# Transposed scores in blocks of 64 keys, masked on the tensor engine, and v weighted in 64x32 tiles

## The chip, the core and the metric

The kernel runs on one core of a Trainium2 chip. The core has a tensor engine (PE) that multiplies matrices out of SBUF into the banks of PSUM, a vector engine (DVE), a scalar engine (ACT), a general engine (POOL), a queue that issues transfers (SP), and 16 DMA engines. All run on their own and wait for each other by semaphores. The metric is the device time of one launch in microseconds, lower is better.

## What is computed

One transformer block over 8 batches of 512 tokens with 128 features: layer norm, then causal attention with 16 heads of 8 features, and beside it a mixture of 8 experts (2 per token, 176 hidden features each) with a shared expert of 352 hidden features. All sums are added to the tokens.

```python
xn = _layernorm(x, axis=-1)
# attention, H = 16 heads of 8 features, S = 512
q, k, v = (to_heads(q), to_heads(k), to_heads(v))
scores = jnp.einsum('bhqd,bhkd->bhqk', q * scale, k) + causal_bias
attn = jax.nn.softmax(scores, axis=-1)
out = jnp.einsum('bhqk,bhkd->bhqd', attn, v) ... @ w_out.T + b_out
# experts: top 2 of 8 by softmax of xn @ gate_w.T, weights scaled by 2.5
g = jax.nn.silu(jnp.einsum('td,edf->etf', x, w_gate)) * jnp.einsum('td,edf->etf', x, w_up)
y = jnp.einsum('te,etd->td', combine, jnp.einsum('etf,efd->etd', g, w_down))
return x + attention(xn) + y + shared(xn)
```

## The kernel before

Each engine has its instructions written out in a fixed order. The batches 1 to 6 are a loop on each engine, batch 0 and 7 are written beside it. A batch `b` has two stages, which the engines pass one after the other:

**The expert stage** (`experts_and_maxima`) has 14 tiles of hidden features, `k` = 0 to 13. For each tile PE computes gate and up (`gate_up`, 6 matmuls of 512 columns, L537 to L539), ACT the silu (L871), POOL the routing weight (L1016), DVE the product (`hidden`, L1229), ACT and POOL the split into two parts (L878, L1024), and PE `down` (3 matmuls, L553 to L555). Between the tiles stand 18 units `pair(b, n)`: scores of queries by keys in 64x64 tiles of the array (`head_scores`, L573), with the causal mask added on PE by 4 more matmuls (`mask_scores`, L564), from which DVE takes the negative row maximum (`maxima`, L1253). Units 0 to 6 share one pair of PSUM banks, so that unit n+1 waits for the maximum of unit n. The maxima go into the operand `q_op` as further rows, so that the transposed scores come out with the maximum subtracted. At `k` = 2 and 3 stand the pieces that end the attention of the batch before: `transpose_o` (L684), `normalise_o` (L1298, L1300), `transpose_on` (L691), `project_out` (L697), `add_attention` (L1315).

**The attention stage** (`attend`). PE computes the scores transposed, keys by queries (`scores_t`, L646), in units of two PSUM banks, 1024 columns of 128 rows. There are 4 groups of 4 heads with 5 units each, 20 in all. A unit has 2 or 4 matmuls in 64x128 tiles: two heads in the two halves of the rows, 128 keys, and the queries from the first of these keys to 511. ACT takes the exponential of each unit from PSUM to `probs` in SBUF (L934). The units alternate between two pairs of banks, so that unit n waits for the exponential of unit n-2. POOL sets the entries above the diagonal of each 128x128 block to zero (`mask`, L1044, 4 instructions per group). Then PE weights v (`weigh_v`, L673): 4 steps per group, one per block of keys, in the order 512, 384, 128, 256 queries; each step has 4 matmuls in float32 in 128x32 tiles, one head each. One group is weighted behind the scores of the next. A float32 matmul is two instructions in the trace.

The end of the stage overlaps the start of the next: `pair(b+1, 0)` waits for the last exponential but one, `gate_up(b+1, 0)` for the last one, since its banks are those of the scores. On PE the last steps of `weigh_v` stand between `pair` 0, `gate_up` 0, `pair` 1, `gate_up` 1 and `pair` 2. In the same stage PE projects q, transposes y, the routing weights (L510) and the first half of the output (`transpose_o(i, 0)`), and DVE splits q and k, computes the routing weights, takes and normalises the first half of the output (`take_o(i, 0)`, L1291, and `normalise_o(i, 0)`) and adds the last batch's attention.

v and the router's logits of the next batch are projected at the end of the expert stage (`project_v_and_logits`, L503): 4 matmuls with 128x128 weights and 136 columns.

## Time and profile before

| | |
|---|---|
| median of 3 runs | 576.67 us (576.14 to 577.02) |
| profiled execution, its own time | 575.52 us |
| span of the profiled execution | 573.8 us |
| PE busy | 522.2 us (91%) |
| DVE busy | 452.5 us (79%) |
| ACT busy | 344.8 us (60%) |
| POOL busy | 322.3 us (56%) |
| granted clock of PE | 0.994 |

The page gives busy times over the whole span. The two stages have different limits, so that the stages are read apart. From 148 us on the kernel repeats itself: the first exponential of a batch starts at 210.27 us and that of the next batch at 276.99 us, so a batch takes 66.72 us. The rows below are mostly from this one batch. In a timeline row the numbers are the start and the length in us; the distance from one start to the next on PE is what a piece costs, since the recorded lengths of matmuls overlap.

### The profile page before, as it was taken

To read this page: it belongs to the slowest core of one execution; us is meant where nothing else is said; L and a number is where in the kernel's file an instruction comes from. 1 tells how busy PE (TensorE), PEld (TensorE's weight loads), DVE (VectorE), ACT (ScalarE), POOL (GpSimd) and SP (SyncE) were. 2 spreads that over 40 slices of the span, in tenths; PEclk is the share of its full clock that TensorE was granted. 3 is DMA by queue.
4 is the path that set the end of the run, shared out by engine and by line. 5 is a ranking of instruction groups with operands and counts; after the bars stand their busy time and mean duration, and the time that the engine had idled before them with its cause. 6 is when DMAs were issued, how large, how long until landed. Compare 5 with 4: busy or idle time off the path is not lost.

```text
span 573.8 us, 13133 instructions
## 1 busy us (share of the span) xinstructions
PE 522.2 (91%) x4536; PEld 295.5 (51%) x4536; DVE 452.5 (79%) x852; ACT 344.8 (60%) x463; POOL 322.3 (56%) x345
## 2 busy tenths in 40 slices
PE   2679999989999999999999999999999999999985
PEld 1345633656346752576436662466525764366522
DVE  5989798897869968797868968699687978589604
ACT  6422597355963479434983469634794349734693
POOL 2036743775447835479255864478355782558552
PEclk9899999999999999999999999999999999999999
DMA  8984037500475006900268004740069003580001
GB/s 269 267 221 114 12 125 206 132 2 9 146 198 138 2 11 194 261 22 0 104 181 200 0 9 153 220 104 0 22 184 261 18 0 119 164 207 1 10 1 37
DMA packets 45405, 61.99 MB, mean 108 GB/s; under 512 B 4960, under 2 KB 28992, under 8 KB 45376
## 3 DMA queue, kind: packets, MB, share of 16 engines
q1 hardware_dynamic: 42668, 58.37, 36.2%
q10 hardware_dynamic: 2708, 3.24, 1.9%
q8 instruction: 18, 0.29, 0.2%
q14 instruction: 11, 0.09, 0.1%
HBM read 45.21 MB, written 15.34 MB: 106 GB/s over the span
## 4 chain that ended last, share of the span: by engine, by line
PE 60%; DVE 13%; ACT 11%; issue 8%; POOL 5%; DMA 2%; ACTq 1%; POOLq 0%; DVEq 0%
PE banks L673 10%; ACT probs L934 8%; PE banks L537 7%; PE banks L538 6%; PE banks L539 6%; PE banks L573 6%; PE banks L553 6%; PE banks L646 6%; DVE neg_max L1253 5%; PE banks L555 3%; PE banks L554 3%; POOL hid_lo L1024 2%; DVE probs L1229 2%; POOL probs L1044 1%; POOL probs L1016 1%
## 5 line engine op out<-in xcount | busy, mean ns | idle before, releaser
L1253 DVE TENSOR_REDUCE neg_max<-banks 128x2 f32<-128x1024 f32 (+7 forms) x240 | 178.3, 794 | 17.2 <-PE banks L564 16.8
L934 ACT ACTIVATE probs<-banks 128x1024 f32<-128x1024 f32 x160 | 155.4, 1031 | 11.4 <-PE banks L646 9.2
L1044 POOL TENSOR_SCALAR_AFFINE_SELECT probs<-probs 128x512 f32<-128x512 f32 x128 | 90.8, 732 | 124.0 <-ACT probs L934 124.0
L1016 POOL TENSOR_TENSOR probs<-probs,cb 128x512 f32<-128x512 f32 x88 | 113.2, 1286 | 81.4 <-ACT probs L871 80.9
L871 ACT ACTIVATE probs<-banks 128x512 f32<-128x512 f32 (+1 forms) x112 | 67.0, 598 | 134.2 <-PE banks L539 133.9
L1024 POOL TENSOR_TENSOR hid_lo<-probs,hid_hi 128x512 fp32r<-128x512 f32 x85 | 109.6, 1290 | 36.6 <-ACT hid_hi L878 36.3
L1229 DVE TENSOR_TENSOR probs<-probs,banks 128x512 f32<-128x512 f32 (+1 forms) x112 | 76.4, 683 | 35.8 <-POOL probs L1016 27.7
L537 PE MATMUL banks<-x_hi,w_hi 128*128 128x512 f32 (+1 forms) x224 | 95.0, 424 | 4.4 <-DVE probs L1229 4.4
L673 PE MATMUL banks<-probs,v_op 128*32 128x512 f32 (+3 forms) x1024 | 95.2, 444 | 3.7 <-POOL probs L1044 3.5
L538 PE MATMUL banks<-x_lo,w_hi 128*128 128x512 f32 (+1 forms) x224 | 89.0, 398 | 0.0
L539 PE MATMUL banks<-x_hi,w_lo 128*128 128x512 f32 (+1 forms) x224 | 88.8, 396 | 0.0
L878 ACT ACTIVATE hid_hi<-probs 128x512 fp32r<-128x512 f32 (+1 forms) x96 | 60.4, 629 | 43.4 <-DVE probs L1229 43.3
L646 PE MATMUL banks<-q_op,k_op 64*128 64x384 bf16 (+3 forms) x512 | 62.8, 302 | 11.6 <-ACT probs L934 11.3
L573 PE MATMUL banks<-k_op,q_op 64*64 64x448 bf16 (+7 forms) x1024 | 54.2, 293 | 9.8 <-DVE neg_max L1253 7.0
L553 PE MATMUL banks<-hid_hi,wd_hi 128*128 128x512 f32 (+1 forms) x112 | 55.3, 493 | 4.2 <-POOL hid_lo L1024 3.6
L646 PEld LDWEIGHTS banks<-q_op,k_op 64*128 64x128 bf16 x512 | 17.4, 94 | 79.9 <-ACT probs L934 57.4
L537 PEld LDWEIGHTS banks<-x_hi,w_hi 128*128 128x128 f32 (+1 forms) x224 | 42.0, 187 | 20.6 <-DVE probs L1229 5.4
L539 PEld LDWEIGHTS banks<-x_hi,w_lo 128*128 128x128 f32 (+1 forms) x224 | 42.0, 188 | 10.7
L538 PEld LDWEIGHTS banks<-x_lo,w_hi 128*128 128x128 f32 (+1 forms) x224 | 42.1, 188 | 7.8 <-issue 0.2
L573 PEld LDWEIGHTS banks<-k_op,q_op 64*64 64x64 bf16 x1024 | 21.0, 105 | 46.8 <-issue 44.6
L555 PE MATMUL banks<-hid_lo,wd_hi 128*128 128x512 f32 (+1 forms) x112 | 44.7, 399 | 0.0
L554 PE MATMUL banks<-hid_hi,wd_lo 128*128 128x512 f32 (+1 forms) x112 | 44.4, 396 | 0.0
(136 smaller groups left out, 552.3 us busy)
## 6 DMA issues: line engine op xcount, KB each, us to landing
cb<-c_dram SPq DMA_DIRECT2D x31, 256.0 KB, 3.9
q_op<-q_dram SPq DMA_DIRECT2D x15, 512.0 KB, 6.8
k_op<-k_dram SPq DMA_DIRECT2D x15, 512.0 KB, 8.2
cb<-c_dram SPq DMA_DIRECT2D x16, 224.0 KB, 4.3
q_dram<-q_parts SPq DMA_DIRECT2D x8, 384.0 KB, 2.5
k_dram<-k_parts SPq DMA_DIRECT2D x8, 384.0 KB, 2.5
cb<-c_dram SPq DMA_DIRECT2D x16, 192.0 KB, 4.2
cb<-c_dram SPq DMA_DIRECT2D x15, 160.0 KB, 4.3
```

The lines of the kernel that those rows point to most:

```text
L537: pe.matmul(bank, w_hi[:, w, cols], x_hi[:, :], start=True, stop=False)
L538: pe.matmul(bank, w_hi[:, w, cols], x_lo[:, :], start=False, stop=False)
L539: pe.matmul(bank, w_lo[:, w, cols], x_hi[:, :], start=False, stop=True).then_inc(ready, 1)
L553: pe.matmul(bank_y[:, :], wd_hi[0:n, tile, :], hi, start=(k == 0), stop=False)
L573: pe.matmul(bank[rows, a, at:at + n], q_op[own, 2 * g + c, HALF * jq:HALF * (jq + 1)], k_op[own, 2 * g + c, 0:n], start=first, stop=False, ...
L646: mm = pe.matmul(bank[:, at:at + S - kb * P], k_op[r:r + HALF, h // 2, kb * P:(kb + 1) * P], q_op[r:r + HALF, h // 2, kb * P:S], start=Tru ...
L673: mm = pe.matmul(bank[32 * j:32 * j + 32, kb * P:S], v_op[:, kb, g % 2, 4 * (g // 2) + j, :], probs_of(g, j, kb), start=(c == 0 and g % 2 ...
L934: nc.scalar.activation(probs[:, g % 2, 2 * u:2 * u + 2, :], ring[:, at:at + 2, :], ACT.Exp).then_inc(exp_done, 1)
L1016: nc.gpsimd.tensor_tensor(sg[k % 3][:, :], sg[k % 3][:, :], cb[:, tiles_of(b)[k], :], ALU.mult).then_inc(weighted, 1)
L1024: nc.gpsimd.tensor_tensor(hid_lo[0:n, k % 3, :], hid[k % 3][0:n, :], hid_hi[0:n, k % 3, :].bitcast(F32), ALU.subtract).then_inc(hid_lo_don ...
L1044: return nc.gpsimd.affine_select(out=view, in_=view, compare_op=ALU.is_ge, fill=0.0, base=0, pattern=[[0, 4], [1, P]], channel_multiplier=-1)
L1253: return nc.vector.tensor_reduce(out, in_, AX.X, ALU.max, negate=True)
```

## The change

Transposed scores. A unit now holds 64 keys instead of 128 for each head, for two pairs of heads at once, in 64x64 tiles: (a, c) are the halves of the array's rows and columns, and 4 heads of one group lie in one unit of two banks. Key blocks w and 8-w share a unit, so a group has 4 units, and every two groups share a ninth: 18 units per batch instead of 20, of 1024 columns each as before. A unit has 4 or 8 matmuls and then 4 more that add the causal mask (`mask_scores_t`). POOL's masking (L1044) is gone, with its semaphore.

Weighting v. A step is one block of 64 keys for the 8 heads of two groups: 8 matmuls in 64x32 tiles, 4 in each half of the rows, into both output banks. The widths of the 8 steps of two groups are 512, 448, 64, 384, 128, 320, 192 and 256 queries, 16 steps per batch as before. A step follows two score units behind the one that holds its keys. `probs` is a ring of 12 units instead of two buffers of 10 blocks.

What follows from this. v is projected with the two halves of the heads in the two halves of the columns (16 matmuls of 128x64 weights and 64 or 72 columns instead of 4), and placed by POOL in 2 copies instead of 4. Both halves of the output are complete only after the last step, so `take_o(i, 0)`, `transpose_o(i, 0)` and `normalise_o(i, 0)` move to the places of their second halves, and `transpose_on` moves behind `gate_up(b, 3)`. The last batch ends with both halves in `last_take_o`, `last_transpose_o` and `last_normalise_o`. The weights of v, the bias of v and the output weights are loaded with 2, 1 and 4 more transfers. `att` shares the memory of `o_norm`.

```diff
+ST_ALL = NAT_ALL
+WEIGHINGS = OWN_UNITS + 1
+PV_ALL = GROUPS // 2 * WEIGHINGS
+WEIGH_BEHIND = 2
+FIRST_WEIGHING = 4
...
-                for a in range(2):
-                    bank = ring[:, 2 * ((n + 1) % 2) + a, :]
...
-                    for h, kb, at in parts:
-                        r = half(h)
-                        mm = pe.matmul(bank[:, at:at + S - kb * P],
-                                       k_op[r:r + HALF, h // 2, kb * P:(kb + 1) * P],
-                                       q_op[r:r + HALF, h // 2, kb * P:S], start=True, stop=True)
+                apart(pe, pe_passed)
+                blocks = keys_of(n)
+                for m, (g, jk, at) in enumerate(blocks):
+                    for c in range(2):
+                        for a in range(2):
+                            pe.matmul(ring[half(c), 2 * ((n + 1) % 2) + a, at:at + S - HALF * jk],
+                                      k_op[half(a), 2 * g + c, HALF * jk:HALF * (jk + 1)],
+                                      q_op[half(a), 2 * g + c, HALF * jk:S], start=(m == 0), stop=False,
+                                      tile_position=(HALF * a, HALF * c), skip_group_check=True)
+                for c in range(2):
+                    for a in range(2):
+                        mm = mask_scores_t(ring[half(c), 2 * ((n + 1) % 2) + a, :], a, c, blocks)
...
-                for j in range(4):
-                    mm = pe.matmul(bank[32 * j:32 * j + 32, kb * P:S], v_op[:, kb, g % 2, 4 * (g // 2) + j, :],
-                                   probs_of(g, j, kb), start=(c == 0 and g % 2 == 0), stop=(c == 3 and g % 2 == 1),
-                                   tile_position=(0, 32 * j), skip_group_check=True)
+                for c in range(2):
+                    for j in range(4):
+                        x, a = j // 2, j % 2
+                        mm = pe.matmul(nat[32 * j:32 * j + 32, c, HALF * jk:S], v_op[half(c), jk ^ c, t, j, :],
+                                       probs[half(c), 2 * home_of(units[x]) + a, at[x]:at[x] + S - HALF * jk],
+                                       start=(t == 0 and jk == 0), stop=(t == 1 and jk == JQ // 2),
+                                       tile_position=(HALF * c, 32 * j), skip_group_check=True)
...
-                for q in range(QT):
-                    mm = pe.matmul(vl[:, q // 2, q % 2, :], xnT[:, q * P:(q + 1) * P], wvg_sb[:, :],
-                                   start=True, stop=True)
+                for jk in range(JQ):
+                    for c in range(2):
+                        at = jk ^ c
+                        n = VG if at % 2 == 0 else E // 2
+                        mm = pe.matmul(vl[half(c), at // 4, at % 4, 0:n], xnT[:, jk * HALF:(jk + 1) * HALF],
+                                       wvg_sb[:, c, 0:n], start=True, stop=True, tile_position=(0, HALF * c),
+                                       skip_group_check=True)
...
                     if k == 2:
+                        transpose_o(i, 0)
                         transpose_o(i, 1)
+                    if k == 3:
+                        transpose_on(i)
...
                     if k >= 2:
                         down(b, k - 2, i)
-                    if k == 2:
-                        transpose_on(i)
...
-            def mask(view):
...
-                return nc.gpsimd.affine_select(out=view, in_=view, compare_op=ALU.is_ge, fill=0.0, base=0,
-                                               pattern=[[0, 4], [1, P]], channel_multiplier=-1)
...
                     if k == 2:
+                        normalise_o(i, 0)
                         normalise_o(i, 1)
                     for m in range(PAIRS_AT[k]):
                         if k == 1 and m == 1:
+                            take_o(i, 0)
                             take_o(i, 1)
```

Three places show how the instructions move; the names are those of the two sources, and their line numbers differ. The first is PE at the end of the attention stage in the loop. Before, in the older source's lines, with L646 the transposed scores, L673 the weighting of v and L573 with L564 the first unit of the next batch's maxima:

```order
L646 MATMUL banks<-q_op,k_op 128x256 x4
L664 REGISTER_ALU
L673 MATMUL banks<-probs,v_op 32x512 x4
L664 REGISTER_ALU
L673 MATMUL banks<-probs,v_op 32x384 x4
L588 ISA
L596 REGISTER_ALU
L573 MATMUL banks<-k_op,q_op 64x512 x4
L564 MATMUL banks<-mask_half,ident_half 64x64 x4
```

And the same place after, where L683 and L696 are the transposed scores and their mask, L713 the weighting, L615 and L606 the maxima's unit:

```order
L683 MATMUL banks<-q_op,k_op 64x256 x8
L696 MATMUL banks<-ident_half,mask_half 64x2x64 x4
L713 MATMUL banks<-probs,v_op 32x128 x8
L630 ISA
L638 REGISTER_ALU
L615 MATMUL banks<-k_op,q_op 64x512 x4
L606 MATMUL banks<-mask_half,ident_half 64x64 x4
```

Two long steps of weighting (512 and 384 queries) stood between the last scores and the next batch's first unit; now one short step does. The second place is PE behind `gate_up(b, 0)`. Before:

```order
L539 MATMUL banks<-x_hi,w_lo 128x512
L664 REGISTER_ALU
L673 MATMUL banks<-probs,v_op 32x128 x4
L601 ISA
L573 MATMUL banks<-k_op,q_op 64x448 x4
L573 MATMUL banks<-k_op,q_op 64x64 x4
L564 MATMUL banks<-mask_half,ident_half 64x128 x4
```

After:

```order
L581 MATMUL banks<-x_hi,w_lo 128x512
L713 MATMUL banks<-probs,v_op 32x320 x8
L713 MATMUL banks<-probs,v_op 32x192 x8
L702 REGISTER_ALU
L713 MATMUL banks<-probs,v_op 32x256 x8
L643 REGISTER_ALU
L615 MATMUL banks<-k_op,q_op 64x448 x4
```

Three steps stand there where one did, and the step of 256 queries that stood behind `gate_up(b, 1)` is gone. The third place is DVE in tiles 1 and 2 of the expert stage, with the maxima (L1253), the copy of the output (L1291) and its normalisation (L1298, L1300). Before:

```order
L1290 REGISTER_ALU
L1291 COPY o_sb<-banks 128x512
L1249 REGISTER_ALU
L1253 TENSOR_REDUCE neg_max<-banks 128x2 x2
L1223 REGISTER_ALU
L1229 TENSOR_TENSOR probs<-probs,banks 128x512
L1297 REGISTER_ALU
L1298 RECIPROCAL o_rden<-banks 128x32
L1300 TENSOR_TENSOR o_norm<-banks,o_rden 128x16x16
```

After, where the same operations are L1311, L1273, L1249, L1319 and L1321:

```order
L1310 ISA
L1311 COPY o_sb<-banks 128x512 x2
L1269 REGISTER_ALU
L1273 TENSOR_REDUCE neg_max<-banks 128x2 x2
L1243 REGISTER_ALU
L1249 TENSOR_TENSOR probs<-probs,banks 128x512
L1317 ISA
L1319 RECIPROCAL o_rden<-banks 128x32
L1321 TENSOR_TENSOR o_norm<-banks,o_rden 128x16x16
L1317 REGISTER_ALU
L1319 RECIPROCAL o_rden<-banks 128x32
L1321 TENSOR_TENSOR o_norm<-banks,o_rden 128x16x16
```

Two copies and two normalisations stand where one of each did; the first of each has left the attention stage.

## Rows read from the trace of the kernel before

**Rows 1.** ACT's timeline in one batch; [idle before it <- who ended it]
```profile
210.27 1.02 ACT L934 ACTIVATE probs<-banks 128x1024 f32<-128x1024 f32 x1 [0.57 <-PE banks L646]
213.99 0.70 ACT L849 ACTIVATE qk_f<-banks,bq_scaled 128x512 f32<-128x512 f32 x1
214.56 14.70 ACT L934 ACTIVATE probs<-banks 128x1024 f32<-128x1024 f32 x15
229.51 1.94 ACT L934 ACTIVATE probs<-banks 128x1024 f32<-128x1024 f32 x2 [0.24 <-PE banks L646]
```

**Rows 2.** PE's timeline, one group of five score units inside the attention stage
```profile
220.52 0.39 PE L646 MATMUL banks<-q_op,k_op 64*128 64x512 bf16 x2 [0.46 <-ACT probs L934]
220.84 1.06 PE L673 MATMUL banks<-probs,v_op 128*32 128x512 f32 x8
221.83 0.39 PE L646 MATMUL banks<-q_op,k_op 64*128 64x512 bf16 x2
223.26 0.42 PE L673 MATMUL banks<-probs,v_op 128*32 128x128 f32 x8
223.62 0.40 PE L646 MATMUL banks<-q_op,k_op 64*128 64x384 bf16 x4
```

**Rows 3.** PE's timeline from the last scores to the second tile's gate
```profile
231.86 0.85 PE L673 MATMUL banks<-probs,v_op 128*32 128x384 f32 x8 [0.50 <-POOL probs L1044]
232.64 0.41 PE L573 MATMUL banks<-k_op,q_op 64*64 64x512 bf16 x4
233.01 0.50 PE L537 MATMUL banks<-x_hi,w_hi 128*128 128x512 f32 x1
234.60 0.43 PE L673 MATMUL banks<-probs,v_op 128*32 128x128 f32 x8
234.96 0.41 PE L573 MATMUL banks<-k_op,q_op 64*64 64x448 bf16 x8
235.36 0.50 PE L537 MATMUL banks<-x_hi,w_hi 128*128 128x512 f32 x1
```

**Rows 4.** PE's timeline, tiles 2 to 4
```profile
239.41 0.60 PE L684 MATMUL banks<-ident_sb,o_sb 128*128 128x128 f32 x4
242.21 0.41 PE L573 MATMUL banks<-k_op,q_op 64*64 64x512 bf16 x4 [0.48 <-DVE neg_max L1253]
246.76 0.50 PE L537 MATMUL banks<-x_hi,w_hi 128*128 128x512 f32 x1
```

**Rows 5.** DVE's timeline in tile 2
```profile
240.05 0.35 DVE L1298 RECIPROCAL o_rden<-banks 128x32 f32<-128x32 f32 x1
240.78 1.28 DVE L1253 TENSOR_REDUCE neg_max<-banks 128x2 f32<-128x640 f32 x2
```

**Rows 6.** PE's timeline, two units for the maxima in a row
```profile
248.35 0.41 PE L573 MATMUL banks<-k_op,q_op 64*64 64x320 bf16 x8
248.65 0.39 PE L573 MATMUL banks<-k_op,q_op 64*64 64x256 bf16 x8
```

**Rows 7.** PE's timeline, the projection of v and what follows it
```profile
275.54 1.09 PE L503 MATMUL banks<-wvg_sb,xnT 128*128 128x136 f32 x8
276.56 0.39 PE L646 MATMUL banks<-q_op,k_op 64*128 64x512 bf16 x2
```

**Rows 8.** The last batch's end, timelines of ACT, PE and DVE
```profile
545.60 15.61 ACT L934 ACTIVATE probs<-banks 128x1024 f32<-128x1024 f32 x16
563.81 1.81 PE L673 MATMUL banks<-probs,v_op 128*32 128x384 f32 x24 [0.51 <-POOL probs L1044]
565.69 0.76 DVE L1332 COPY o_sb<-banks 128x256 f32<-128x256 f32 x2 [2.43 <-PE banks L673]
```

**Rows 9.** SP's timeline at the start; the last row is from the list of transfers
```profile
2.40 0.43 SPq L345 DMA_DIRECT2D wvg_sb<-in_gateT  x1
6.47 1.28 SPq L352 DMA_DIRECT2D probs<-in_ident  x2
...
probs<-in_ident SPq DMA_DIRECT2D x2, 16.0 KB, 7.0
```

More of the change, by code:

```diff
@@ L189, in block_kernel @@
         ident_f = early[:, after + HALF:after + 2 * HALF]
[L191 to L192 removed]
+        hid = [probs[:, 2 * n, :] for n in (LEFT - 2, LEFT - 1, LEFT - 3)]
+        sg = [probs[:, 2 * n + 1, :] for n in (LEFT - 2, LEFT - 1, LEFT - 3)]
         yT = o_sb[:, 0, :]
@@ new lines, in scores_t @@
+                apart(pe, pe_passed)
+                blocks = keys_of(n)
+                for m, (g, jk, at) in enumerate(blocks):
+                    for c in range(2):
+                        for a in range(2):
[3 more added lines that the diff above has]
+                                      tile_position=(HALF * a, HALF * c), skip_group_check=True)
@@ new lines, in scores_t, with mask_scores_t @@
+                for c in range(2):
+                    for a in range(2):
+                        mm = mask_scores_t(ring[half(c), 2 * ((n + 1) % 2) + a, :], a, c, blocks)
+                mm.then_inc(st_ready, 1)
+            def mask_scores_t(bank, a, c, blocks):
+                second = blocks[-1][2] // HALF
+                diagonal = bank.rearrange("p (k n) -> p k n", n=HALF)[:, 0:second + 1:max(second, 1), :]
+                return pe.matmul(diagonal, mask_half[half(a), :],
+                                 ident_half[half(a), :].unsqueeze(1).to_broadcast([HALF, len(blocks), HALF]),
+                                 start=False, stop=True, tile_position=(HALF * a, HALF * c), skip_group_check=True)
@@ new lines, in weigh_v @@
+            def weigh_v(i, t, w, part, front):
+                pe.wait_ge(exp_done, ST_ALL * i + last_unit_of(t, w) + 1)
+                if t == 0 and w == 0 and part == 0:
+                    pe.wait_ge(v_placed, i + 1)
+                    if front:
+                        pe.wait_ge(q_done, i + 2)
+                        pe.wait_ge(k_done, i + 2)
+                apart(pe, pe_passed)
+                jk, units, at = weighing_of(t, w)[part]
+                for c in range(2):
+                    for j in range(4):
[4 more added lines that the diff above has]
+                                       tile_position=(HALF * c, 32 * j), skip_group_check=True)
+                if part == len(weighing_of(t, w)) - 1:
@@ L863, in silu @@
                 if k == 0:
-                    before(act, pv_done, 0 if isinstance(b, int) and b == 0 else GROUPS * b - 1)
+                    before(act, pv_done, 0 if isinstance(b, int) and b == 0 else PV_ALL * b - WEIGHINGS)
                 act.wait_ge(gate_ready, NT * b + k + 1)
@@ L904, in experts @@
                             take_xT(b + 1)
+                    if k == 3 and i is not None:
+                        act.wait_ge(onT_ready, i + 1)
+                        nc.scalar.activation(o_normT[:, :], nat[:, 0, :], ACT.Copy).then_inc(onT_done, 1)
                     if i is None and k == 1:
@@ L911, in experts @@
                         square_root(1)
-                    if k == 2 and i is not None:
-                        act.wait_ge(onT_ready, i + 1)
-                        nc.scalar.activation(o_normT[:, :], nat[:, 0, :], ACT.Copy).then_inc(onT_done, 1)
             def take_y(i):
```

261 lines of the change are left out of this document (119 added, 142 removed).

## Prediction

> **What bounds the kernel now.** I read the busy times first. PE is busy 91% of the span, but a busy PE is not one whose speed counts in each stage, so the timelines of one batch come next, one engine after the other. In the attention stage ACT's row of fifteen exponentials takes 14.70 us, 0.98 us each with no gap, and before it ACT waits little [rows 1]. PE waits for ACT once in each group of five score units, 0.46 us here [rows 2]. So ACT sets the pace there, with PE close behind: a group takes five exponentials, 4.9 us, and with one wait of 0.46 us in it PE has 4.4 us of work. At the end of the stage it is not ACT any more. The last exponential ends at 231.45 [rows 1], while the first gate matmul, which needs nothing else of ACT, starts at 233.01: a wait of 0.50 us for POOL's mask, a step of weighting and the first unit for the maxima stand before it on PE [rows 3]. In the expert stage PE and DVE are both full. PE waits for DVE once, 0.48 us, at the unit of the maxima in tile 2 [rows 4]. So a batch of 66.72 us has about 1.9 us of ACT's pace to gain from two exponentials less, some 1.5 us at the end of the stage, and little cover for new PE or DVE work.
>
> **Scores and their mask.** Before, a unit costs PE 0.32 us (220.52 to 220.84) [rows 2]. After, a unit is the same set of instructions as a unit for the maxima, 4 or 8 matmuls in 64x64 tiles and 4 for the mask, which costs 0.37 and 0.40 us with the change of tiling in it (232.64 to 233.01, 234.96 to 235.36) [rows 3]; without that change it is 0.30 [rows 6]. Of 18 units 4 are short: 4 x 0.37 + 14 x 0.40 = 7.1 us per batch against 20 x 0.32 = 6.4, so +0.7. The cost is well covered by rows, the lower end would be 18 x 0.30 = 5.4.
>
> **Weighting v.** Before, a step of 512 queries costs 0.99 us (220.84 to 221.83) and one of 128 costs 0.36 (223.26 to 223.62) [rows 2]: 1.64 ns per query and 0.15 us fixed. A batch has 4 x 1280 = 5120 queries in 16 steps, 8.4 + 2.4 = 10.8 us. After, a step has 8 matmuls in 64x32 tiles. No row shows float32 in such tiles. If all eight stream at once, as the four of a unit for the maxima do, the cost per query stays, and there are 2 x 2304 = 4608 queries in 16 steps. I take 0.17 us fixed, near the 0.15 of the nearest row and a little more for twice the instructions: 7.6 + 2.7 = 10.3 us, so -0.5. The lower end is 0.05 fixed (the change of tiling nearly free, -1.9 more), the upper ends are rivals 2 and 3 below.
>
> **The attention stage.** What counts is when the last exponential ends. The fifth score unit starts at about 214.7, beside the fourth exponential (214.56) [rows 1]. From there to the end of the last scores PE now has 14 units (12 x 0.40 + 2 x 0.37 = 5.54), 12 steps with 3712 queries (6.09 + 12 x 0.17 = 8.13) and the turning of the routing weights (0.3): 13.97 us, to 228.7. With 0.2 us to ACT and 1.03 for the exponential the stage ends at 229.95. ACT alone would be done at 214.56 + 14 x 0.98 + 1.03 = 229.3. So **PE takes over as the bound**, by 0.6 us, and 1.5 of the 1.96 us of the two exponentials are left. POOL's masks, 16 instructions per batch, are off the path but for the 0.50 us before [rows 3]. Behind the last scores PE has one step of 128 (0.36) and the first unit (0.37), done at 229.5, so that the gate starts 0.2 us after the last exponential, at 230.15 instead of 233.01: **-2.85 us**.
>
> **The start of the expert stage** gives most of it back. PE: gate and up of tile 0, 1.59 us (233.01 to 234.60) [rows 3], to 231.75; three steps of weighting, 768 queries, 1.26 + 0.51 = 1.77, to 233.5, where one of 0.36 stood (and one of 256 later, 0.57, is gone); unit 1, gate and up of tile 1 and unit 2, 0.40 + 1.59 + 0.40, to 235.9; gate and up of tile 2, 1.49, to 237.4. DVE meanwhile: the maxima of unit 1 from 234.0, 1.2 us; then two copies of the output instead of one, 0.6 each, to 236.4; the maxima of unit 2, to 237.6; the product of tile 1, to 238.2. PE's transposes of the output start at 237.4, and the first reciprocal follows 0.64 us later as now (239.41, 240.05) [rows 4, 5], at 238.05 by PE and at 238.2 by DVE. Two normalisations instead of one take 2 x 0.73 (240.05 to 240.78) [rows 5], so that the next maxima start at 239.7 and unit 4 starts 1.43 later as now (240.78 to 242.21) [rows 4, 5], at 241.1 instead of 242.21: -1.1. `transpose_on` stood in the shadow of this wait; behind the gate of tile 3 it costs PE its 0.5. What is left at tile 4 is **-0.6 us**.
>
> **The projection of v** costs 1.02 us now (275.54 to 276.56) [rows 7] and stands between the last tiles, where every microsecond of PE counts. After, it has four times the instructions of half the width, in two column tiles. If the two overlap it costs the same, if not 2.0 us. I take +0.3, nearer to the first, since tiles of one unit overlap everywhere else. A batch then changes by -0.3 us, and seven passages from one attention stage through the next expert stage by -2.1.
>
> **Both ends.** In the last batch PE's sum is the same without the routing weights: from 546.65 (545.60 and the first exponential of that row) [rows 8] 13.67 us to 560.3, then four steps, 896 queries, 1.47 + 0.68, to 562.5, and DVE's copy at 562.7 instead of 565.69 [rows 8]: -3.0. The copies, transposes and normalisations behind it now cover both halves of the output; the copies alone go from 0.76 to about 1.2, the rest adds 0.8, so -1.7. At the start three more transfers stand in SP's queue ahead of the last constants, 0.5 us each (0.43 to 0.64) [rows 9]. These now land at 7.1 + 7.0 = 14.1 [rows 9], and would at 15.7, about when DVE wants them. I take +0.5, between 0 and the full 1.6. Sum: -2.1 - 1.7 + 0.5 = -3.3. Against the profiled execution's own 575.52 that is 572.2; this execution was 1.15 below the median of the runs, so against the median 576.67 it is **573.4 us**.
>
> **Rivals.**
> 1. PE keeps up with ACT. If changing between 64x64 and 64x32 is nearly free, the attention stage ends at ACT's 229.3, 0.65 earlier, and the three steps behind the gate cost 0.36 less: -1.0 more per batch, -7.4 in all, 566. Against it: each change of tiling before costs about 0.1 on either side (0.40 and 0.30 for one unit) [rows 3, 6].
> 2. Slower: short steps cost what their instructions cost. Twelve matmuls with no change of tiling take 0.30 us, 25 ns each [rows 6], though that is mostly their 640 columns. If 16 instructions cannot go below 0.40, steps of 64, 128 and 192 queries cost 0.55 instead of 0.28, 0.38 and 0.48. Five of these stand in PE's path per batch, +0.85, with the end +6.8: 580. It decides for slower as soon as the fixed part of a step passes 0.19 us, since 15 steps per batch are on PE's path. The Trainium skill, TensorEngine Tiling (Array Packing), section Instruction Overhead, has the same floor, about 60 cycles a matmul however few columns; by it an estimate of the sum comes to the same 580, and by the rows' line alone to 573.4.
> 3. Far slower: the eight tiles do not run at once. A float32 matmul is two instructions for one tile, and four tiles at once means that three second halves wait while later first halves start. With eight tiles seven must wait. If PE looks no further ahead than now, the second half of the rows starts with the second pass and a step takes three passes instead of two: 0.82 ns more per query, 4480 queries on the path, +3.7 per batch, +30 in all, 603. For it speaks only that no row shows eight; against it, that starts of four tiles go round in turn in 64x64 and in 128x32 alike.
> 4. The start of the expert stage gives all back (units 3 and 4 wait longer for DVE, whose queue got 1.35 us more there), or the projection of v costs its upper end of +1.0: -0.6 + 1.0 = +0.4 per batch, 575.5 to 578.3.
> 5. By strict order of the tiles a step of 512 would now take five half passes, 2.1 us, and 0.99 is what the rows show [rows 2]. The Trainium skill, TensorE: Matmul & The Clock Gate, section Part 3: Packing small matmuls, says that matmuls start in strict order with no reordering. The trace disagrees. If the rule held for more than four tiles, a step would be nine half passes instead of two, 26 us more per batch and about 750 us in all.
>
> **How the numbers follow.** Forecast (571 to 576.5) 0.43, rival 1 0.15, rival 2 0.19, rival 3 0.10, rival 4 0.12, rival 5 0.01. A measurement of this kernel tells about 0.2%, 1.2 us, from no change. Faster is rival 1 and most of the forecast, 0.52; slower is rivals 2, 3 and 5 and half of rival 4, 0.35; the rest, 0.13, is no change. The range 565 to 583 leaves out rivals 3 and 5 and the far ends.
>
> **What would show it.** In the profile after: exponentials with small gaps, no more released by ACT alone, and ending some 1.5 us earlier relative to the first; score units at 0.40 and a step of 512 at about 1.0 us on PE's timeline; a step of 64 at 0.28 (forecast) or 0.55 (rival 2); the first gate about 19.9 us after the first exponential instead of 22.7; a longer wait for the maxima at unit 4, above 1 us instead of 0.48; the projection of v at 1.3. The forecast is wrong if a step of 512 takes 1.4 us, if the expert stage is longer than now by over 2.9 us, or if the start of the program moves by more than 1.5.

## The result and the profile after

The change makes the kernel **slower**: 626.40 us median of 4 runs (625.29 to 626.87) against 576.61 us for the kernel before (576.14 to 577.02), a ratio of 1.086 (95% interval 1.084 to 1.088). The forecast was 573.4 us. The profiled execution took 626.87 us, 625.1 of them the span. Here and below medians and ranges are of all executions of a kernel, ratios and their intervals of the fast ones alone, and the profiled execution of `a_two` is a slow one.

The page of the kernel after: busy time of the engines; TensorE's granted clock in 40 slices; the queue that loads instructions (packets, MB, share); the chain that ended last.

```profile
PE 544.5 (87%) x6840; PEld 325.0 (52%) x6840; DVE 432.1 (69%) x851; ACT 330.8 (53%) x447; POOL 229.8 (37%) x201
PEclk9889999999789988999889999899989899799998
q8 instruction: 64, 1.05, 0.7%
PE 64%; DVE 15%; issue 10%; ACT 4%; DMA 3%; POOL 3%; SPq 1%; DVEq 0%; ACTq 0%
```

PE's matmuls grow from 4536 to 6840, and yet PE is busy for a smaller share of the span. The chain has 10% "issue": time in which PE waits for nothing that the profile shows. The instruction queue q8 had 18 packets of 16 KB before and has 64 now; its line on the page before:

```profile
q8 instruction: 18, 0.29, 0.2%
```

A row of lines says where the "issue" stands (groups of PE, whole run; the last part is idle time ahead of them):

```profile
L713 PE MATMUL banks<-probs,v_op 64*32 64x512 f32 (+7 forms) x2048 | 97.4, 443 | 6.5 <-issue 6.5
L683 PE MATMUL banks<-q_op,k_op 64*64 64x512 bf16 (+7 forms) x1024 | 64.0, 317 | 8.5 <-issue 7.8 <-DMA q_op<-max_rows 0.4 <-ACT probs L979 0.3
L696 PE MATMUL banks<-ident_half,mask_half 64*64 64x128 bf16 (+1 forms) x576 | 34.7, 226 | 18.7 <-issue 18.7
```

All three are lines of the attention stage; the idle time marked "issue" ahead of them is 33 us together. One stage on PE's timeline, and ACT's beside it:

```profile
224.26 0.41 PE L683 MATMUL banks<-q_op,k_op 64*64 64x448 bf16 x6 [1.73 <-issue]
...
236.88 1.09 PE L713 MATMUL banks<-probs,v_op 64*32 64x512 f32 x16
237.90 0.41 PE L683 MATMUL banks<-q_op,k_op 64*64 64x384 bf16 x8
242.26 0.32 PE L696 MATMUL banks<-ident_half,mask_half 64*64 64x128 bf16 x4 [3.95 <-issue]
...
243.51 1.74 PE L713 MATMUL banks<-probs,v_op 64*32 64x448 f32 x16
...
242.71 1.95 ACT L979 ACTIVATE probs<-banks 128x1024 f32<-128x1024 f32 x2 [4.64 <-PE banks L696]
```

PE stops in the middle of a score unit, between its score matmuls and its masks. No semaphore stands there. ACT starves for 4.64 us. When PE goes on its clock is at the lower level: the 448 step takes 1.7 us where it takes 0.9 at full clock (below). The list of transfers for 239.0 to 241.5, inside the stop, has one load of instructions; PE goes on 1.4 us after it has landed (240.87):

```profile
q8 instruction: 1, 0.02, 3.3%
```

Two passes of the loop as windows (start:end, length, busy time and instructions of PE, of its weight loads, of DVE, ACT and POOL, granted clock, DMA share, GB/s), cut at the first and the last of the third `down` matmuls of a batch (L597; L555 before): the attention stage is from the last of one batch to the first of the next.

```profile
296.90:332.10 35.20, 29.59 (x521) 14.32 (x520) 18.98 (x43) 21.82 (x26) 2.85 (x3) 0.90 0.56 158
332.10:371.00 38.90, 37.28 (x336) 25.90 (x335) 32.21 (x56) 18.20 (x29) 25.88 (x22) 1.00 0.16 40
```

The same two windows of the kernel before:

```profile
278.70:307.60 28.90, 27.00 (x269) 10.78 (x268) 22.48 (x45) 23.18 (x28) 14.09 (x19) 1.00 0.68 191
307.60:345.40 37.80, 37.06 (x301) 25.79 (x299) 31.56 (x54) 18.31 (x29) 26.37 (x24) 1.00 0.15 38
```

Cut in this way, the 51.3 us by which the span grew are: 35.9 in the seven attention stages (203.4 to 239.3), 13.2 in the eight expert stages, 1.8 ahead of the first `down`, and 0.5 behind the last.

PE's program in 64-byte instructions explains the q8 count. Before it has 4755, of which 1239 (77 KB, in 6 blocks of 256) are the loop that runs five times; the trace has no q8 load between 204 and 484 us. After it has 7167, of which 1830 (114 KB, 7.15 blocks) are the loop, and nine loads come in the pass from 296.9 to 371.0. The traces bear the two sizes out: 1238 and 1829 instructions of PE from one branch back to the next.

### The profile page after: what moved, and what is told of

The parts are those of the page before. It is cut to its first block, busy times and chain, and to the rows that moved or that the text cites. A ratio compares the mean times of both kernels' runs of the same rounds, so it can differ in the third digit from the quotient of the medians.

```text
span 625.1 us, 17566 instructions
## 1 busy us (share of the span) xinstructions
PE 544.5 (87%) x6840; PEld 325.0 (52%) x6840; DVE 432.1 (69%) x851; ACT 330.8 (53%) x447; POOL 229.8 (37%) x201
## 4 chain that ended last, share of the span: by engine, by line
PE 64%; DVE 15%; issue 10%; ACT 4%; DMA 3%; POOL 3%; SPq 1%; DVEq 0%; ACTq 0%
PE banks L713 13%; PE banks L683 8%; DVE neg_max L1273 7%; PE banks L579 6%; PE banks L581 5%; PE banks L580 5%; PE banks L595 5%; PE banks L615 5%; PE banks L596 3%; PE banks L597 3%; ACT probs L979 2%; POOL hid_lo L1068 2%; DVE probs L1249 2%; PE banks L533 2%; PE banks L696 2%
## 5 line engine op out<-in xcount | busy, mean ns | idle before, releaser
L1273 DVE TENSOR_REDUCE neg_max<-banks 128x2 f32<-128x1024 f32 (+7 forms) x240 | 178.1, 792 | 40.7 <-PE banks L606 40.5
L979 ACT ACTIVATE probs<-banks 128x1024 f32<-128x1024 f32 x144 | 141.2, 1027 | 63.2 <-PE banks L696 63.1
L713 PE MATMUL banks<-probs,v_op 64*32 64x512 f32 (+7 forms) x2048 | 97.4, 443 | 6.5 <-issue 6.5
L1249 DVE TENSOR_TENSOR probs<-probs,banks 128x512 f32<-128x512 f32 (+1 forms) x112 | 76.2, 681 | 38.5 <-POOL probs L1060 27.7
L581 PE MATMUL banks<-x_hi,w_lo 128*128 128x512 f32 (+1 forms) x224 | 90.6, 404 | 0.0
L683 PE MATMUL banks<-q_op,k_op 64*64 64x512 bf16 (+7 forms) x1024 | 64.0, 317 | 8.5 <-issue 7.8
L615 PE MATMUL banks<-k_op,q_op 64*64 64x448 bf16 (+7 forms) x1024 | 55.3, 296 | 17.6 <-DVE neg_max L1273 13.9
L683 PEld LDWEIGHTS banks<-q_op,k_op 64*64 64x64 bf16 x1024 | 21.1, 109 | 80.0 <-issue 78.1
L696 PE MATMUL banks<-ident_half,mask_half 64*64 64x128 bf16 (+1 forms) x576 | 34.7, 226 | 18.7 <-issue 18.7
L615 PEld LDWEIGHTS banks<-k_op,q_op 64*64 64x64 bf16 x1024 | 21.2, 106 | 53.9 <-issue 51.7
L597 PE MATMUL banks<-hid_lo,wd_hi 128*128 128x512 f32 (+1 forms) x112 | 44.2, 395 | 0.0
```

The costliest lines, as they stand in the source:

```text
L581: pe.matmul(bank, w_lo[:, w, cols], x_hi[:, :], start=False, stop=True).then_inc(ready, 1)
L615: pe.matmul(bank[rows, a, at:at + n], q_op[own, 2 * g + c, HALF * jq:HALF * (jq + 1)], k_op[own, 2 * g + c, 0:n], start=first, stop=False, ...
L683: pe.matmul(ring[half(c), 2 * ((n + 1) % 2) + a, at:at + S - HALF * jk], k_op[half(a), 2 * g + c, HALF * jk:HALF * (jk + 1)], q_op[half(a) ...
L713: mm = pe.matmul(nat[32 * j:32 * j + 32, c, HALF * jk:S], v_op[half(c), jk ^ c, t, j, :], probs[half(c), 2 * home_of(units[x]) + a, at[x]: ...
L979: nc.scalar.activation(probs[:, 2 * home_of(n):2 * home_of(n) + 2, :], ring[:, at:at + 2, :], ACT.Exp).then_inc(exp_done, 1)
L1249: nc.vector.tensor_tensor(hid[k % 3][0:n, :], sg[k % 3][0:n, :], ring[0:n, up_bank(k), :], ALU.mult).then_inc(hid_done, 1)
```

## The experiments

**Theory A:** PE's longer loop no longer stays loaded; it is loaded again in each pass, and PE stops for it, with a lower clock behind each stop. **Theory B:** the code has no part in it; the new matmuls, their tiles and increments cost the time.

**More instructions in the kernel before.** `b_pad7` and `b_pad16` put 7 or 16 increments ahead of each score unit of PE's loop:

```
+                for _ in range(7):          # or 16
+                    pe.sem_inc(pe_passed, 1)
```

> The kernel before, unchanged in its work, with 7 semaphore increments that nobody waits for ahead of each of PE's 38 score units inside the loop: the loop body of PE grows from 1239 to 1504 instructions (77 to 94 KB). Theory A (the change makes PE's loop too long to stay loaded, so that it is loaded again in each pass, and PE stands still for it): 1504 still fit, no q8 loads inside the loop, time within 1% of before (575 to 582 us). Theory B (the new matmuls, their tiles and increments cost the time, and PE's code has nothing to do with it): increments are cheap, 576 to 582 us. This one is the control for the next.

> As the last, with 16 increments ahead of each of the 38 units: PE's loop body is 1846 instructions (115 KB), as long as that of the changed kernel (1830), and the work is that of the kernel before. Theory A: q8 loads come in each pass of the loop as in the changed kernel (about 8), PE stops for 1 to 4 us at some of them where nothing hides it: 585 to 620 us. Theory B: no stops; at most twice what the increments of the last run cost, 577 to 590 us.

Measured: 602.9 us (ratio 1.046, 1.043 to 1.049) and 849.7 us (1.474, 1.469 to 1.478). The instruction queue of the two, and an attention stage of each:

```profile
q8 instruction: 19, 0.31, 0.2%
290.50:323.80 33.30, 27.75 (x269) 10.89 (x268) 22.29 (x45) 24.07 (x28) 13.88 (x19) 1.00 0.70 189
```

```profile
q8 instruction: 57, 0.93, 0.5%
385.20:451.30 66.10, 42.47 (x269) 13.24 (x268) 20.30 (x43) 24.64 (x28) 14.18 (x19) 0.61 0.39 105
```

The counts are as theory A has them: 1504 instructions in 7 blocks stay loaded, 1846 in 8 blocks don't. The times are not usable for it. Both expectations took an increment to be cheap, and it is not. In either trace they follow each other every 151 ns on PE's queue, here ten of them (count, length in ns, first and last start in us):

```profile
L482 PEldq EVENT_SEMAPHORE  x10: 51/51/51, 403.0 to 404.4; - x10
```

With seven ahead of a unit part of that is hidden: the 147 of the stage shown lengthen it by 4.4 us (33.3 against 28.9), 30 ns each. The 355 of the other stage lengthen it by 37 us, 105 ns each, with stops of 0.3 to 2.2 us ahead of most units, one of 5.3, and a mean clock of 0.61. So the padding itself spoils the sum, and both theories' times were missed.

**Fewer instructions, and where the loop stands.** `a_two` has two mask matmuls a unit instead of four, each 128 columns of weights wide; `a_two_al` is the same with the loop's head at the start of a block:

```
-                for c in range(2):
-                    for a in range(2):
-                        mm = mask_scores_t(ring[half(c), 2 * ((n + 1) % 2) + a, :], a, c, blocks)
+                for a in range(2):
+                    mm = mask_scores_t(ring[:, 2 * ((n + 1) % 2) + a, :], a, blocks)
...
+            pe.addr_align(256, offset=0, max_nops=0)      # a_two_al alone
             with pe.Fori(1, NB - 2) as i:
```

> The changed kernel with two mask matmuls a score unit instead of four, each over 128 rows (the 64 columns of the mask and of the identity stand twice): PE's loop body falls from 1830 to 1686 instructions (6.6 blocks of 256, which lie across 8 blocks), the whole program from 7167 to 6591. Theory A: 8 blocks are touched in each pass, so the loads stay, but a little fewer stops: 612 to 626 us. Theory B: shorter by the masks alone, at most 38 units x 7 batches x 2 matmuls x 30 ns = 16 us, 610 to 626 us.

> As the last, instruction for instruction, with the head of PE's loop put at the start of a block, so that its 1686 instructions touch 7 blocks and not 8. Theory A: if 7 blocks stay loaded, the loads inside the loop go, with the stops and the half clock behind them: 575 to 600 us, well below the last. If the loads stay all the same, A needs a smaller limit, and the time is that of the last. Theory B: same as the last, 610 to 626 us.

Measured: 632.4 us (1.095, 1.091 to 1.099) and 605.0 us (1.050, 1.048 to 1.052). One pass of the loop of each, as one window (the profiled execution of `a_two` took 639.95 us, the longest of its four, that of `a_two_al` 603.11, the shortest, so that the rows differ by more than the medians do), with its instruction queue (the aligned kernel has none in its passes; its row is that of the page):

```profile
q8 instruction: 9, 0.15, 0.8%
305.00:382.50 77.50, 70.73 (x785) 39.75 (x783) 51.69 (x98) 40.54 (x55) 28.53 (x24) 0.96 0.33 92
```

```profile
q8 instruction: 26, 0.43, 0.3%
291.80:361.60 69.80, 67.87 (x784) 39.30 (x783) 51.54 (x98) 39.97 (x55) 28.53 (x24) 1.00 0.36 100
```

The two run the same instructions on data of the same place. Moving the loop by less than a block takes 27 us away, with all loads in the loop, all stops over 1.2 us in it that have no releaser, and the low clock. **Theory B falls**. 605 us is above A's range (575 to 600) as well, and 632.4 is above both theories' ranges for `a_two`. What both had left out is a price of the masks: a unit now costs 0.51 us (226.40 to 226.91) instead of 0.40, so that 36 units cost some 3.6 us a batch, 25 us in all. That prices the rest of the way from 605 down to 580.

```profile
226.40 0.41 PE L681 MATMUL banks<-q_op,k_op 64*64 64x384 bf16 x8
226.75 0.23 PE L693 MATMUL banks<-ident_half,mask_half 64*128 64x128 bf16 x2
226.91 0.61 PE L710 MATMUL banks<-probs,v_op 64*32 64x448 f32 x8
```

**The changed kernel, its loop moved or made to fit.** `a_al` is the changed kernel with that one `addr_align` line. `a_res` has 1780 instructions in the loop:

```
+TWO_MASKS = (0, 1, 2, 3)                # maxima units with two masks, the rest four
+TWO_MASKS_T = (0, 1, 2, 3, 4, 5, 6)     # the same for transposed units
...
-                pe.wait_ge(exp_done, ST_ALL * i + last_unit_of(t, w) + 1)
+                if part == 0:           # likewise around its apart(...)
+                    pe.wait_ge(exp_done, ST_ALL * i + last_unit_of(t, w) + 1)
```

> The changed kernel with nothing but the head of PE's loop put at the start of a block of 256 instructions. Its 1830 instructions are 7.15 blocks and still touch 8. Theory A (the loop reloads its code because it touches 8 blocks, and 7 stay loaded): loads stay, 615 to 635 us. Rival C (the gain of the aligned kernel with two masks came from where the head stands and not from the number of blocks): as good as there, about 27 us faster than the changed kernel, 595 to 602 us.

> The changed kernel with its loop cut to 1780 instructions and put at the start of a block, so that it touches 7 blocks; four masks a unit stay in 14 maxima units and 11 transposed units, two masks in the other 4 and 7; the second part of a weighting step goes without its own wait and increment, which the first part has. Theory A with the prices of my prediction: no loads, no stops, full clock, and the 0.10 us that a unit with two masks costs more (11 of them, 1.1 us a batch) : 573.4 + 8 = 581 us, range 576 to 588. If the aligned kernel's 605 us had another cause than its masks (36 units x 0.10 us x 7 = 25 us), it stays at 598 to 605 us.

Measured: 589.95 us (585.7 to 603.1; ratio 1.024, 1.019 to 1.029) and 578.85 us (1.007, 1.004 to 1.010). `a_res` lands where A and the forecast's own prices put it. `a_al` contradicts what A expected of it (loads in each pass, 615 to 635 us) and comes nearer to rival C (595 to 602), though below it. C is right in that the place of the head decides here, with eight blocks touched in both kernels; but the gain comes with the end of the loads, as A has it. The page's q8 row, and the two stages of the third pass, in the profiled execution, the shortest of its four:

```profile
q8 instruction: 37, 0.61, 0.4%
288.30:315.20 26.90, 26.43 (x521) 13.44 (x520) 18.94 (x42) 21.26 (x26) 2.82 (x3) 1.00 0.69 192
315.20:354.20 39.00, 37.36 (x337) 25.87 (x335) 32.24 (x56) 18.31 (x29) 25.96 (x22) 1.00 0.20 46
```

In its second pass nine loads come, with a stop of 2.27 us at the branch back; in the three passes after that none. So eight blocks are held too if the loop begins with one, at least in this execution; the others, of up to 603 us, were not traced. Why eight don't stay when the head is in the middle (10.43 to 17.58 blocks from the start by the count of the compiled program; in the trace the first branch back is PE's instruction 4468, 17.45 blocks) is not settled by these runs. A loop that is loaded again takes one load more than the blocks it touches: nine for eight in the changed kernel, `a_two` and `b_pad16`, eleven for ten in `b_spread` below. So one block beyond the loop seems to be fetched too, but no run tests that.

The page "Advanced Engine Details and Errata" of the Trainium skill, section ISA Cache, gives TensorE 128 KB in lines of 16 KB, which is 8 lines of 256 instructions. The packets of q8, 16 KB each, and the eight blocks that stay in `a_al` agree with it; that eight don't stay in the changed kernel doesn't follow from it. The same section says "Only 2 cache lines!", and there the traces disagree, since six, seven and eight blocks stayed.

**The kernel before, its loop spread out.** `b_spread` goes on at the start of the next block at nine places of the loop, so that the 1239 instructions touch 10 blocks; `b_branch` has branches at the same places over at most 15 slots:

```
+                    if spreading[1] % 4 == 0:
+                        pe.addr_align(256, offset=0, max_nops=0)     # b_branch: 16
```

> The kernel before, same instructions, with PE's loop cut at nine places: at each the code goes on at the start of the next block, behind a branch, so that its 1239 instructions lie in 10 blocks and not in 6. Theory A: about 10 q8 loads in each pass where there was none, PE stops where nothing hides them, 600 to 650 us. Theory B: nine branches a pass and nothing more, 576 to 582 us.

> Control of the last: the same nine branches at the same nine places, each over at most 15 slots, so that the loop still lies in 6 blocks. Both theories: no loads in the loop, 576 to 582 us.

Measured: 588.4 us (1.020, 1.013 to 1.027) and 575.55 us (0.999, 0.998 to 1.001). So loading the code again makes the kernel before slower as well, by 1.3 to 2.7%, with nine branches more in its loop that cost nothing by themselves (`b_branch`). But it costs less than A expected: eleven loads a pass (the transfers of one pass), and only the one behind the branch back is waited for in each pass.

```profile
q8 instruction: 11, 0.18, 1.2%
285.42 0.40 PE L656 MATMUL banks<-q_op,k_op 64*128 64x384 bf16 x4 [1.81 <-issue]
```

That opens a question: why do the other loads lie hidden here, while the changed kernel has a second, longer stop in each attention stage? The windows above hold a difference: before, 269 matmuls (each with a weight load, 538 instructions) fill 28.9 us, 54 ns an instruction; after, 521 fill 26.9, 26 ns. The expert stages have 63 and 58 ns.

**No loop at all.** `a_flat` and `b_flat` write the five passes out (`for i in range(1, NB - 2)` for PE alone), 14190 and 9334 instructions:

> The changed kernel with the five passes of PE's loop written out one after the other (the other engines keep their loops): 14190 instructions of PE instead of 7167, the same work in the same order, and no branch back. Every block is now loaded once, 55 in all. Theory A1 (PE stops because of the branch back: after it the next block is asked for too late): the loads lie hidden beside the work, no stop over 1 us in the attention stages, batches of 65.9 us as in the aligned kernel's passes without loads: 566 to 576 us. Theory A2 (this stage's code is used up faster than any load can follow, loop or not): stops of 3 to 5 us in each attention stage as before, 610 to 640 us. Theory B (the code has no part in it): 626 us.

> The kernel before with PE's loop written out in the same way, 9334 instructions instead of 4755: the control. A1 and B: as before, 575 to 578 us. A2: a little slower at the most, since its stages have a third fewer instructions, 576 to 585 us.

Measured: 606.4 us (602.1 to 609.0; 1.051, 1.045 to 1.057) and 577.2 us (1.001, 0.999 to 1.002). A1 is wrong, A2 is right in kind, its range (610 to 640) a little too high: without any branch the changed kernel still has one long stop in each attention stage but the first and the last, of 4.63, 4.54, 3.22, 3.42, 2.54 and 3.11 us (1.35 in the last). The stop at 235.06, in three windows:

```profile
228.00:235.10 7.10, 7.06 (x180) 2.87 (x173) 4.20 (x16) 6.66 (x8) 0.00 (x0) 1.00 0.67 186
235.10:239.60 4.50, 0.00 (x0) 0.00 (x0) 2.29 (x4) 0.51 (x1) 0.00 (x0) 0.72 0.49 127
239.60:246.00 6.40, 5.92 (x109) 1.99 (x108) 0.42 (x1) 4.12 (x5) 0.00 (x0) 0.67 0.85 249
```

In the 7.1 us ahead of the stop no instruction load starts; PE issues 353 instructions there, more than a block. The load that it needs starts at 237.23, 2.2 us after PE has stopped. In five of the six stops the load starts 0.5 to 2.2 us behind the start of the stop, in the sixth just ahead of it. The section Instruction fetch mechanics of "Runtime: NRT & Kernel Launch" in the Trainium skill says that crossing a block of 16 KiB is mostly hidden and that a taken branch to code that isn't there breaks the prefetch. For the kernel before the runs agree with both (no stop over 1 us in `b_flat`, 1.81 to 2.07 us behind each branch back in `b_spread`); the first half does not hold in this stage.

**Does a pause let the load go out?** `a_flat_w` and `a_w` (in the loop) make PE wait in three units a stage for the exponential just before:

```
-                    pe.wait_ge(exp_done, ST_ALL * i + n - 1)
+                    pe.wait_ge(exp_done, ST_ALL * i + n - 1 + int(n in (6, 10, 14)))
```

> The written-out changed kernel (606.4 us), and in each attention stage PE waits at transposed units 6, 10 and 14 for the exponentials of the unit just before, not of the one before that: three short pauses of PE a batch, about 1 us each, same work. Theory D (PE's code runs out where its instructions follow one another so closely, 424 in 8.3 us, that the request for the next block goes out only after PE has stopped; a pause lets it go out): the stop of 2.5 to 4.6 us in each attention stage and the half clock behind it go, 3 us of pauses come: attention stages of 28.5 to 30.5 us and 580 to 595 us in all. Rival E (the load comes when it comes, by the number of instructions or for a reason outside this engine): the stops stay and the pauses are added, 610 to 630 us.

> The changed kernel itself, in its loop (626.4 us), with the same three pauses. Theory D: the long stop of each attention stage (3.3 to 4.5 us, and the half clock behind it) goes, that after the branch back (1.7 to 2.0 us) stays, since it does not depend on how closely instructions follow: 595 to 612 us. Rival E: 630 to 645 us.

Measured: 610.7 us (1.062, 1.060 to 1.064) and 638.7 us (1.113, 1.106 to 1.120). Both times lie in rival E's ranges (610 to 630 and 630 to 645), not in D's. But E has the stops stay, and in the written-out kernel they shrink: PE's idle time marked "issue" falls from 23.4 us to 11.1 from the first attention stage on, while its waits for ACT's exponentials grow from 2.7 to 20.0. The trace of `a_flat_w` shows two kinds of stage. In one the load starts 0.5 us after a pause begins (241.14; load 241.63 to 242.96), too late to be in time, and the stop that is left is 1.69 us instead of 4.54; in the other (from 306.26) both loads come early and no stop is over 0.55 us:

```profile
242.22 0.41 PE L683 MATMUL banks<-q_op,k_op 64*64 64x384 bf16 x8 [1.08 <-ACT probs L979]
...
244.38 0.21 PE L696 MATMUL banks<-ident_half,mask_half 64*64 64x128 bf16 x1 [1.69 <-issue]
...
314.18 0.41 PE L683 MATMUL banks<-q_op,k_op 64*64 64x384 bf16 x8 [1.08 <-ACT probs L979]
```

So a load that is due does go out soon after PE's stream of instructions pauses, twice in this trace 0.5 us after. That speaks for theory D, but the pauses cost more than they save, by 4 us here and by 12 in the loop, and the first attention stage, which had no such stop, now has one of 2.94. As a mechanism D is made likely, not shown: where in the sequencer the request is held up can't be seen in these records.

**DVE's start, and the best that came of it.** `a_flat_s` and `a_res_s` scale the q bias after the first split of x:

```
-            dve.wait_ge(qk_weights, 16 * 2)
-            nc.vector.tensor_scalar(bq_scaled[:, :], bqk[:, 0:1], QSCALE, None, ALU.mult).then_inc(const_made, 1)
             low_shared()
             split_x(0, nat[:, 0, :])
+            dve.wait_ge(qk_weights, 16 * 2)
+            nc.vector.tensor_scalar(bq_scaled[:, :], bqk[:, 0:1], QSCALE, None, ALU.mult).then_inc(const_made, 1)
```

> As the written-out changed kernel, and DVE scales the q bias after it has split the first tokens, not before: at the start DVE stood 2.68 us for the q and k weights (0.92 in the kernel before), since SP now issues four transfers for the v weights ahead of them. If that wait carries to the end of the program: 1.5 to 3 us less than the written-out kernel without it. If q and k, whose projections need the same weights, are late all the same: no difference over 0.5 us.

> The changed kernel in 7 blocks with fewer concessions: the weighting steps go without waits that an earlier one already gives, so that 1790 instructions remain with two masks only in maxima units 0 to 3 and transposed units 0 to 2; head of the loop at the start of a block; and the change at DVE's start of the last kernel. Against 578.9 us of the first kernel in 7 blocks: 4 transposed units x 0.10 us x 7 = 2.8 less for the masks, 1.5 to 3 less for the start: 572 to 575 us, which would be below the kernel before by 0.2 to 0.7%. If the start gives nothing, 575 to 577.

Measured: 608.6 us (601.6 to 613.3) against 606.4 (602.1 to 609.0) for `a_flat`, no gain that can be told apart. In the profiled executions it is there at first: the last `down` of batch 0 starts at 75.3 us instead of 77.2. Behind it the stops of the attention stages differ by more than that from stage to stage. `a_res_s` took 576.1 us median (573.1 to 579.6, ten runs), ratio 0.9995 (0.997 to 1.002): **no difference from the kernel before**, as in the second of the two sums. Its loop gains in each pass, and the first expert stage loses it in the profiled execution:

```profile
285.10:351.40 66.30, 64.50 (x842) 39.43 (x841) 51.20 (x98) 39.54 (x55) 28.76 (x24) 1.00 0.39 105
29.70:79.80 50.10, 45.21 (x356) 28.00 (x355) 40.50 (x67) 17.84 (x28) 24.83 (x21) 0.88 0.37 96
```

A pass takes 66.3 us against 66.7. The first expert stage runs at a mean clock of 0.88 and takes 50.1 us, where the kernel before has 45.7 at 0.98. It begins behind a wait of PE for the first keys' transfer, 2.50 us here and 2.42 before. How long the low clock lasts there differs between kernels with the same instructions in that stage (48.3 us in `a_al`, 47.1 in the changed kernel, 45.5 in `a_flat`; 47.9 in `b_flat` against 45.7 in the kernel before), and these runs don't say why.

## Why the prediction was wrong

**The step that failed** is the sum of a batch, "-0.3 us, and seven passages ... by -2.1": its terms are the durations and the waits of PE's instructions, and the loading of PE's code, which isn't among them, was put at nothing without a reason. In the pass shown above a batch of the changed kernel takes 74.1 us instead of 66.7, which is +7.4. The number was at hand: the matmuls of a batch grow from 569 to 857, and the page before has its row of q8. No rival held it either; all five were about the durations and the order of matmuls and the waits for DVE. What the runs showed in its place: 27 us for moving the loop by part of a block (`a_two` to `a_two_al`), 36 us for the same in the changed kernel (`a_al`), 47.5 us for making it fit with small concessions (`a_res`). Which loads are waited for is less clear: that PE's dense instructions hold back the request for the next block (theory D) stays open.

Point by point, against the third pass of `a_al`, which has the changed kernel's instructions and no loads (PE's and ACT's timelines):

```profile
286.58 1.03 ACT L980 ACTIVATE probs<-banks 128x1024 f32<-128x1024 f32 x1 [0.82 <-PE banks L696]
...
301.38 4.91 ACT L980 ACTIVATE probs<-banks 128x1024 f32<-128x1024 f32 x5 [0.43 <-PE banks L696]
306.34 0.50 PE L579 MATMUL banks<-x_hi,w_hi 128*128 128x512 f32 x1 [0.46 <-ACT probs L980]
...
316.99 0.41 PE L615 MATMUL banks<-k_op,q_op 64*64 64x512 bf16 x4 [1.36 <-DVE neg_max L1274]
...
284.97 1.19 PE L544 MATMUL banks<-wvg_sb,xnT 128*64 128x72 f32 x32
286.09 0.41 PE L683 MATMUL banks<-q_op,k_op 64*64 64x512 bf16 x4
```

- **Score units and weighting steps: right.** In the changed kernel's own trace a unit takes 0.40 us and a step of 512 queries 1.02:

```profile
228.58 1.09 PE L713 MATMUL banks<-probs,v_op 64*32 64x512 f32 x16
229.60 0.41 PE L683 MATMUL banks<-q_op,k_op 64*64 64x384 bf16 x8
229.84 0.23 PE L696 MATMUL banks<-ident_half,mask_half 64*64 64x128 bf16 x4
230.00 0.98 PE L713 MATMUL banks<-probs,v_op 64*32 64x448 f32 x16
...
231.31 0.34 PE L713 MATMUL banks<-probs,v_op 64*32 64x64 f32 x16
231.58 0.41 PE L683 MATMUL banks<-q_op,k_op 64*64 64x320 bf16 x8
```

  A step of 64 takes 0.27 us (forecast 0.28, rival 2 0.55), so rival 2 falls; 1.02 for 512 fells rivals 3 (1.4) and 5 (nine half passes, some 3.8; its 2.1 is for the four tiles before). All eight tiles stream at once: eight of the step's matmuls start from 228.58 to 228.63, the other eight from 229.03 to 229.08.
- **The attention stage: right.** The last exponential ends 19.71 us after the first begins (forecast 19.68; before 21.18 [rows 1]) and the gate of tile 0 starts 19.76 after it (forecast 19.9). PE is the bound, as said, and rival 1 falls.
- **The start of the expert stage: right in kind, the give-back too large.** Unit 4 starts 30.4 us after the first exponential, where the forecast had 30.8 and the kernel before 31.9 [rows 1, 4]. Its wait for DVE is 1.36 us (1.50 in the changed kernel), "above 1 us instead of 0.48".
- **The projection of v:** 1.12 us, forecast 1.3, before 1.02 [rows 7]. Rival 4 falls with the last two.
- **A batch:** 65.9 us where the code is resident, forecast 66.4, before 66.7. The mechanism of the change holds; without the loads it gains 0.8 us a batch.
- **The start: mis-sized.** Forecast +0.5 for the last constants. The added transfers stand ahead of the q and k weights too, and DVE waits for those ahead of its first split: 2.82 us instead of 0.92. The first `down` is 1.8 us late.

```profile
13.17 0.15 DVE L1506 TENSOR_SCALAR bq_scaled<-bqk 128x1 f32<-128x1 f32 x1 [2.82 <-DMA wqk_sb<-in_wqkT]
```

- **The tail:** forecast -1.7. Behind the last `down` of batch 7 the changed kernel takes 29.6 us against 29.1, with stops in it; `a_res_s`, without, takes 27.0, which is -2.1.
- **The signs named ahead:** a 512 step of 1.4 us, an expert stage longer by 2.9, a start later by 1.5. The first did not come (1.02), nor the second in the pass shown (+1.1; in two of the eight expert stages a stretch of low clock made it +3.0), the third did by 0.3, and the failure came from outside the list.

## What to carry to other kernels

Count instructions as code, not only as time: if a change adds instructions to a loop, work out the loop's size in blocks of 256 before and after, and look in the profile for the instruction queue, whose packets in the loop should be none. Here six or seven blocks stayed loaded, eight only with the head at a block's start, and a loop that is loaded again cost 2 to 4 us a pass in sparse code and 8 to 11 where short matmuls follow each other at some 26 ns an instruction. A stop marked "issue" in the middle of a run of matmuls, with no wait there, and a low clock behind it are its signs; moving the loop's head costs one line to try.

## What the runs showed of the hardware

- One 16 KB load of PE's code took 0.9 to 1.8 us, and PE went on 1.2 to 1.8 us after it had landed. A load that was waited for cost 1.0 to 5.1 us of stop in all.
- Writing a loop out does not cure it: with 14190 instructions in a row, each block loaded once, six of the eight attention stages still had a stop of 2.5 to 4.6 us (`a_flat`).
- A stop of 4.5 us (`a_flat`, 235.1 to 239.6) was followed by 6.4 us at a mean clock of 0.67, between the levels of 1.2 and 2.4 GHz; in the changed kernel an attention stage of 35.2 us has 5.2 us of stops and 3 us more from the clock.
- Increments of a semaphore that are instructions of their own on PE's queue followed each other every 151 ns. Seven ahead of a unit cost 30 ns each in the attention stage (`b_pad7`), sixteen 105 ns each, with loads and a low clock in it (`b_pad16`).
- Two mask matmuls of 64x128 tiles cost a unit 0.1 us more than four of 64x64 (0.51 us in `a_two_al` against 0.40).
